# Cross-attention and mixture-of-experts kernel: GpSimd issues only DMAs beside the experts; a new order of the first turn, the router's first step and the late pieces

## The reference

```python
x = x + xattn(layernorm(x), ctx, Wq, Wk, Wv, Wo)
n = layernorm(x)
idx, w = gate(n)                       # top 4 of 32, by groups
x = x + moe(n, idx, w, w1, w2, w3) + (silu(n @ sg) * (n @ su)) @ sd
```

## Time and profile before

| | us |
|---|---|
| median of 3 runs | 1687.53 (1684.35 to 1688.19) |
| profiled execution | 1686.83 |
| its span | 1685.1 |
| PE, DVE, ACT, POOL busy | 1618.0, 1223.4, 787.4, 887.6 |
| TensorE's mean granted clock | 0.991 |

### The profile page before, as it was taken

One profiled execution on the slowest core, in us unless ns is written; L12 is line 12 of the kernel. 1 busy time (PEld: TensorE's weight loads), 2 busy tenths in 40 slices (PEclk: granted clock), 3 DMA queues, 4 the chain that ended last, 5 costly groups with the idle time before them and its releaser, 6 DMA issues. The chain is left out here.

```text
span 1685.1 us, 34839 instructions
## 1 busy us (share of the span) xinstructions
PE 1618.0 (96%) x12194; PEld 1153.3 (68%) x12194; DVE 1223.4 (73%) x3498; ACT 787.4 (47%) x1986; POOL 887.6 (53%) x1188
## 2 busy tenths in 40 slices
PE   6999999999999999999999999999999999999983
PEld 4767677777777777767676767776776766555541
DVE  6887676767676776767676777777777765787872
ACT  5764444435343444444443544445454433565551
POOL 2444544545463636464545463646455356677773
PEclk9999999999999999999999999999999999999997
DMA  7654433344344434343335544445454385799974
GB/s 233 184 143 79 89 80 80 82 76 96 64 96 76 96 61 92 70 102 67 80 74 97 93 95 92 102 95 108 90 112 83 88 319 155 207 281 281 275 194 59
DMA packets 394461, 204.12 MB, mean 121 GB/s; under 512 B 347808, under 2 KB 356000, under 8 KB 394288
## 3 DMA queue, kind: packets, MB, share of 16 engines
q1 hardware_dynamic: 380416, 180.27, 44.4%
q0 software_dynamic: 13312, 20.57, 6.6%
q10 hardware_dynamic: 560, 1.05, 0.2%
HBM read 87.15 MB, written 31.36 MB: 70 GB/s over the span
## 5 line engine op out<-in xcount | busy, mean ns | idle before, releaser
L961 ACT ACTIVATE arena<-arena,neg_max 128x256 f32<-128x256 f32 x512 | 253.7, 496 | 384.7 <-DVE neg_max L1260 331.5
L690 POOL TENSOR_SCALAR arena<-arena,prob_scale 128x256 f16<-128x256 f32 x384 | 184.5, 496 | 461.2 <-DVE prob_scale L1269 447.1
L1260 DVE CUSTOM_DVE_ANT_0 arena<-ps_score,mask_add 128x256 f32<-128x256 f32 x512 | 186.6, 421 | 141.7 <-PE ps_score L1606 141.7
L1604 PE MATMUL ps_query<-xn_both,arena 128*128 128x256 f16 x1024 | 279.2, 273 | 1.6 <-DMA xn_both<-xn_half 1.6
L1606 PE MATMUL ps_query<-xn_both,arena 128*128 128x256 f16 x1024 | 279.1, 273 | 0.0
L1605 PE MATMUL ps_query<-xn_both,arena 128*128 128x256 f16 x1024 | 279.1, 273 | 0.0
L1275 DVE SCALAR_TENSOR_TENSOR arena<-arena,prob_scale 128x256 f16<-128x256 f32 x384 | 233.0, 654 | 8.2 <-POOL arena L690 8.2
L1604 PE MATMUL ps_out<-arena,o_t 128*128 128x512 f16 x512 | 194.1, 379 | 0.7 <-DVE o_t L1280 0.7
L1605 PE MATMUL ps_out<-arena,o_t 128*128 128x512 f16 x512 | 194.0, 379 | 0.0
L1606 PE MATMUL ps_out<-arena,o_t 128*128 128x512 f16 x512 | 194.0, 379 | 0.0
L745 POOL DMA_INDIRECT slot_table<-entry,slot_at x128 | 133.2, 1041 | 48.2 <-issue 33.4
(11 more groups left out here) (319 smaller groups left out, 4110.7 us busy)
## 6 DMA issues: line engine op xcount, KB each, us to landing
arena<-w SPq DMA_DIRECT2D x96, 512.0 KB
x_in<-x SPq DMA_DIRECT2D x16, 512.0 KB, 4.0
xn_rows<-xn_half SPq DMA_DIRECT2D x15, 512.0 KB, 3.1
out_rows_dram<-x SPq DMA_DIRECT2D x30, 256.0 KB
ctx_in<-ctx_t SPq DMA_DIRECT2D x16, 256.0 KB, 3.1
weight_in<-wq SPq DMA_DIRECT2D x8, 512.0 KB, 5.8
weight_in<-wo SPq DMA_DIRECT2D x8, 512.0 KB, 4.6
arena<-arena SPq DMA_TRANSPOSE x256
```

Of the source, the lines that this page charges most:

```text
L690: pool.tensor_scalar(p_rows[:, c, 0, :], probs[:, c, :], prob_scale[:, c:c + 1], 1.0, ALU.mult, ALU.mult).then_inc(norm_hi, 1)
L961: act.activation(probs[:, c, :], probs[:, c, :], ACT.Exp, bias=neg_max[:, c:c + 1], scale=-1.0, accum_out=prob_sum[:, c:c + 1]).then_inc(e ...
L1260: dve.tensor_tensor_reduce(out=probs[:, c, :], in0=ps_score[h][:, t * S:(t + 1) * S], in1=mask_add[b % 2][:, :], scale=-SCORE_SCALE, scala ...
L1604: pe.matmul(dst, a.hi, b.hi, start=start and n == 0, stop=False)
```

## The change

- GpSimd's `expert_high` is gone. ScalarE makes part 2 as well: for experts 0 to 2 among the late pieces, after that as the last thing of turn e for expert e+2, waiting for `pe_ey` (expert_down(e-1)).
- Beside the experts, the hidden tiles of u pieces are split by ScalarE (`piece_high`, after expert_ht_high) and VectorE (`piece_rest`, after expert_ht_low). GpSimd issues only DMAs there.
- `PIECES` has two u pieces in front of each pair of d pieces instead of one. `EARLY` is 24; the 18 others stand in turns 0 to 6, 8 to 14 and 16 to 19, so shared adds 3 and 4 come in turn 8 and 5 and 6 in turn 20 (before: 10 and 26).
- GpSimd's last scatters of batch 14 (`record(z - 1, 1)`) come after its late splits 0 to 5. Piece 23 stands between expert_rows(0) and expert_rows(1).
- Start: x of batch 0 is loaded in two halves with a semaphore each; ctx_low(0) comes after xn_rest; TensorE makes the first value tile before scores(0); VectorE splits value 0 after prob_scales(0), value 1 and context 1 after key_low(1); weight chunks wq 2, wq 3, ... come one place ahead of wo 0, wo 1, ....
- choose_0 and choose_1 of each batch come after key_low(4) instead of around query_low(4).

```diff
@@ PIECES @@
-    PIECES.append(("u", _n, 0))
+    PIECES += [("u", _n, f) for f in range(2)]
     PIECES += [("d", _n - 1, t) for t in range(TB)] if _n else []
-    PIECES += [("u", _n, f) for f in range(1, FSB)]
+    PIECES += [("u", _n, f) for f in range(2, FSB)]
...
-EARLY = 22
+EARLY = 24
-NOT_BY_POOL = (10, 13, 14, 15, 16)
+NOT_BY_POOL = (10, 11, 14, 15, 16)
...
-    if _e % 4 != 3 and EARLY + len(BESIDE) < len(PIECES):
+    if _e % 8 != 7 and EARLY + len(BESIDE) < len(PIECES):
@@ jobs @@
-                by_rows("wo", wo_s, wo, PAIR, D, 0, 0), by_columns("wq", wq_s, wq, KD, 2, 256, 1),
-                by_columns("wv", wv_s, wv, KC, 1, 512, 2), by_rows("wo", wo_s, wo, PAIR, D, 1, 3),
-                by_columns("wq", wq_s, wq, KD, 3, 256, 0), by_columns("wk", wk_s, wk, KC, 1, 512, 1)]
+                by_columns("wq", wq_s, wq, KD, 2, 256, 0), by_rows("wo", wo_s, wo, PAIR, D, 0, 1),
+                by_columns("wv", wv_s, wv, KC, 1, 512, 2), by_columns("wq", wq_s, wq, KD, 3, 256, 3),
+                by_rows("wo", wo_s, wo, PAIR, D, 1, 0), by_columns("wk", wk_s, wk, KC, 1, 512, 1)]
@@ SP @@
+                if b == 0:
+                    for t, sig in ((0, in_first), (1, in_x[0])):
+                        sp.dma_start(x_in[0][:, t, :], x[t * P:(t + 1) * P, :]).then_inc(sig, 16)
+                    return
@@ GpSimd, after the turns @@
-            record(z - 1, 1)
             for k in range(3):
                 late_split(k)
             inv_std(1, z, x1_stats, x1_rstd, x1_normed)
-            for k in (3, 4):
+            for k in (3, 4, 5):
                 late_split(k)
-            for e in range(2):
-                expert_high(e)
-            for k in range(7, 10):
+            record(z - 1, 1)
+            for k in (8, 9):
                 late_split(k)
             add_shared(0)
...
-            expert_high(2)
+            late_split(17)
...
-            for k in range(19, EARLY):
+            for k in (20, 21):
+                late_split(k)
+            for e in range(3, 5):
+                gather(e)
+            for k in (22, 23):
                 late_split(k)
             add_shared(1)
-            for e in range(3, 5):
-                gather(e)
             add_shared(2)
...
             for e in range(E + 2):
-                if e in BESIDE:
-                    late_split(BESIDE[e])
-                if e >= 1 and e - 1 + HELD < E:
-                    expert_high(e - 1 + HELD)
                 if e + 5 < E:
                     gather(e + 5)
@@ ScalarE @@
+            def piece_high(k):
+                kind, n, at = PIECES[k]
+                if kind == "d":
+                    return
+                u, both = ups(n, at), late_h_t[n % 2]
+                act.wait_ge(hid, u + 1)
+                act.wait_ge(glu_lo, u)
+                act.wait_ge(pe_down, downs(n - 1, 0))
+                act.activation(both.hi[:, at, :], late_hidden[at % 2][:, :], ACT.Copy, scale=1.0).then_inc(glu_hi, 1)
...
+                elif part == 2 and e >= HELD:
+                    act.wait_ge(pe_ey, e - HELD + 1)
...
                     expert_ht_high(e)
+                if e in BESIDE:
+                    piece_high(BESIDE[e])
                 if e + HELD < E:
                     expert_high(e + HELD, 1)
                 if e + 2 < E:
                     copy_rows(e + 2)
                 if e >= 2 and e % 2 == 0:
                     scale_y(e - 2)
+                if HELD <= e + 2 < E:
+                    expert_high(e + 2, 2)
@@ VectorE @@
-            ctx_low(0)
             x_norm(0)
             for t in range(TB):
                 xn_rest(0, t)
+            ctx_low(0)
...
                     maxima(i)
-                if i == 0:
-                    value_low(ps_fill[1], 0, 0, 0)
-                    value_low(ps_fill[0], 0, 0, 1)
-                    ctx_low(1)
...
                     piece(1)
+                if i == 0:
+                    value_low(ps_fill[1], 0, 0, 0)
...
-                if j == 3 and routed:
-                    choose_0(z)
                 if i + 1 < TURNS:
                     query_low(i + 1)
-                if j == 3 and routed:
-                    choose_1()
...
                     key_low(i + 1)
+                if i == 0:
+                    value_low(ps_fill[0], 0, 0, 1)
+                    ctx_low(1)
+                if j == 3 and routed:
+                    choose_0(z)
+                    choose_1()
...
                     expert_ht_low(e)
+                if e in BESIDE:
+                    piece_rest(BESIDE[e])
@@ TensorE @@
+                if i == 0:
+                    filler(("value", 0, 0, 0), ps_fill[1])
                 if i < TURNS:
                     scores(i)
                 if i == 0:
-                    filler(("value", 0, 0, 0), ps_fill[1])
                     filler(("value", 0, 0, 1), ps_fill[0])
...
-            for e in range(2):
-                expert_rows(e)
+            expert_rows(0)
+            piece(EARLY - 1)
+            expert_rows(1)
```

More of the change, by code:

```diff
@@ L1486, in dve_program @@
                     find_slots(z)
-                late_head = i < TURNS and first(b, j) is not None and first(b, j)[0] in ("value", "down")
                 if live:
@@ L1492, in dve_program @@
                     piece(1)
+                if i == 0:
+                    value_low(ps_fill[1], 0, 0, 0)
+                late_head = live and first(b, j) is not None and first(b, j)[0] in ("value", "down")
                 if i and not late_head:
@@ L1541, in dve_program @@
             piece(4)
-            for part in (0, 1, 2):
+            piece(5)
+            for part in (0, 1):
                 expert_low(0, part)
@@ L1546, in dve_program @@
             choose_2()
-            piece(7)
             choose_3()
@@ L1580, in dve_program @@
                 table_scaled, 1)
-            piece(21)
+            for k in (21, 22, 23):
+                piece(k)
             for e in range(E + 1):
@@ L1864, in pe_program @@
             rank(ps_fill[1], z)
[L1865 removed]
+            for k in range(11, EARLY - 1):
                 piece(k)
[L1867 to L1868 removed]
+            expert_rows(0)
+            piece(EARLY - 1)
+            expert_rows(1)
             for e in range(E + 1):
```

63 lines of the change are left out of this document (27 added, 36 removed).

## The result

The changed kernel took 1667.7 us (median of 4 runs, 1664.7 to 1669.1) against 1687.2 for the kernel before (1684.4 to 1688.2): ratio 0.9885, 95% interval 0.9866 to 0.9904. Its profiled execution has a span of 1664.9 and a time of 1666.6. Forecast were 1658.3 and 1660.0. Run again beside the experiments it took 1673.0 (6 runs, 1668.8 to 1676.5), ratio 0.9929 (0.9916 to 0.9942), which is 12 us in place of 20: the two intervals don't meet, so the gain is some 0.7% to 1.15%, and no run says more closely which.

What follows compares the result with a forecast made beforehand. TensorE (busy 96%) was taken to bind, GpSimd's chain of adds from turn 20; -3.1 - 6.0 - 0.8 + 6.8 - 23.7 = -26.8 gave time 1660.0, forecast 1661; 50% 1655 to 1668, range 1646 to 1679.

Steps and rivals of the forecast that it cites:

- First turns, -3.1: First batch's opening turns: reordered VectorE splits bring the second scores 3.3 us earlier, the third turn's 3.1; bounds -5.0 to +1.0.
- The part put at nothing, the start: Before the first scores: the earlier first value and x loaded in two halves were each given no gain.
- Router's first step, -6.0: Fourth turns of the last six batches: choose_0 and choose_1 behind the key remove six 1.0 us waits; bounds -6.0 to 0.
- Late pieces, -0.8: Late pieces to first expert: waits and low clock removed, -6.0; two more pieces, +5.2; net -0.8, bounds -3 to +5.
- Turns 0 to 19, +6.8: Expert turns: three more pieces +6.5, a 3.5 us stall gone, new first-turn wait 3.3, ScalarE's order 0.5; bounds 0 to +22.
- Turns 20 to the end, -23.7: Last expert turns, without pieces: 114.3 us becomes 90.5, bound by GpSimd's chain of adds; bounds 80 to 98.
- 9 + 15 + 9.4 + 20.8 + 24.1 + 12.15: Turn 20 to end: gather and even add, shared adds 5 and 6, one, two, three row-add pairs, tail: 90.5 us.
- A: Last expert turns: the adds keep up, TensorE binds to the end, ten us less, 1651; chance 17%.
- B: Expert turns with a piece: ScalarE binds, 0.9 x 18 = 16 us more, 1677; chance 13%.
- C: Experts: DMA engines become the bound, late loads stop ScalarE's tanh, slower at 1694; chance 8%.
- D: Front parts move nothing, as VectorE or transposes' landing replaces each wait: 9 less gained, 1670; chance 8%.
- E: Experts: GpSimd stays as late, held by its DMAs and landings, not the splits: 1676; chance 4%.

Runs made afterwards that it cites:

- e2: Changed kernel with the first turn's value and second-context splits put back ahead of the probability scales: 1674.1 us, ratio 0.9936 to the kernel before.
- e10: Changed kernel with the third part of each expert's weights loading only an eighth of its columns from expert 9 on: 1663.8 us, ratio 0.9879.
- e1: Changed kernel with only the router's first step (choose_0, choose_1) back where it stood: 1676.2 us, ratio 0.9952 to the kernel before.
- e12: e11 with shared add 5 alone in turn 18, add 6 alone in turn 22, and 26 warming matmuls for 18: 1663.3 us, ratio 0.9848.
- e4: Changed kernel with shared adds 1 and 2 ahead of gathers 3, 4 and late splits 22, 23 on GpSimd: 1666.6 us, ratio 0.9886.
- e3: Changed kernel with the third weight part of experts 3 to 31 back on GpSimd: 1674.8 us, ratio 0.9939 to the kernel before.
- e11: Changed kernel with e4's edit and the 18 pieces beside the experts spread, three in four turns, to turn 22: 1659.8 us, ratio 0.9850.
- e9: Changed kernel with VectorE's split of the first context back ahead of the norm of x: 1671.2 us, ratio 0.9923 to the kernel before.

## Why the prediction was right, and where its sizes were off

*What binds* was read rightly, but for the start: the waits named for the other places are those that the profiles show. The second scores' wait is 1.7, the six waits are gone, GpSimd stands 10.2 us behind shared adds 5 and 6, TensorE waits at turn 24, and 11.9 follow the last pair's first add. The sizes were not: the total came near in part because misses cancel. In the first profile turns 0 to 19 cost 5.0 us more than forecast and the end brought 7.3 less, while the start, batches 10 to 15 and the late pieces brought 5.9 more. The first measurement, 1667.7, is at the slow edge of the 1655 to 1668 given one chance in two, the second, 1673.0, is outside it.

*First turns, -3.1*: measured -2.9 to -3.6 for turns 0 and 1, confirmed by e2. The part put at nothing, the start, is not nothing: -1.2 to +2.7, by the context's landing and by a low clock that the trace of before, at 1.00, did not show. Neither was priced; from the key to the first scores it is 6.4 us at full clock (7.6 in e10, with its 2.5 us wait) and 8.1 to 8.9 where the clock fell.

*Router's first step, -6.0*: -7.0, and e1 gives the same 7.0 back: 1.17 a turn, 0.17 more than the wait that the profile showed.

*Late pieces, -0.8*: -2.7 in every profile but e12's (-2.1). Its first term adds up to 3.95 (2.35 + 1.0 + 1.7 - 1.1), not 4.1. The 1.1 us of waits that I left in did not appear, nor did the 0.5 further on.

*Turns 0 to 19, +6.8*: +7.4 to +11.8 with the same code. Three pieces more cost their 6.5 and the stall of turns 14 to 16 is gone, as worked out. The term that was mis-sized is the wait for shared adds 1 and 2: 3.3 expected, 4.9 idle and 3.1 of low clock found (9.5 on ScalarE). I had counted from gather(4); behind it late splits 22 and 23 (1411.68 to 1414.16) stand ahead of the adds, and all four land only 9.2 after they start. And no price was put on the clock that falls behind a wait of 4 us. e4 takes the term away.

*Turns 20 to the end, -23.7*: -9.8 to -16.4. This is the term that failed in size. Against the sum 9 + 15 + 9.4 + 20.8 + 24.1 + 12.15 stand, in the first profile, 13.0 + 15.7 + 9.4 + 23.0 + 24.9 + 11.9 (1567.03, 1580.04, 1595.74, 1605.10, 1628.09, 1652.98, 1664.9). The links without loads and the tail were right within 1 us. The start of shared adds 5 and 6, the sum's first term, was 4 late here, and with the same code it is 12.6 to 20.3 where 9 was forecast: the even add that turn 19 left began 4.9 into turn 20, not 2.4, and the next followed 8.1 behind it, not 6.5. One pair with gathers took 13.2, not 10.4. For both I had taken landings from rows of the end, where the loads had ended. And the gain's cause was put in part in the wrong place: with the casts back on GpSimd e3 still takes 101.9 for this stage where the kernel before takes 114.3, so 12 us of it don't need GpSimd's relief. That they come from where the pieces and shared adds stand is argued, not isolated by a run.

*Rivals.* A did not come: not even without adds 5 and 6. B, ScalarE at its limit, did not either: in turns 3 to 19 TensorE keeps its 7.18 and 8.38, with one wait of 0.8. C's premise is right and its consequence was not: the DMA engines are 0.96 to 1.03 busy from 1490 to 1600 (above), but TensorE never waits for weights there; what they slow is the adds' landing. D is refuted in the first profile by -2.9 in turns 0 and 1 and -7.0 of the router's step. E is right up to turn 20 (e3). On the page "DMA: Bandwidth & Descriptors" of the Trainium skill, section "Anatomy of one DMA", the fit of 2.0 us plus bytes over 436 GB/s gives an estimated 2.6 us for such an add; measured are 3.1 us for the same rows written and 5.1 added, with idle loads, and the sums go by the measured ones.

## What to carry to other kernels

Price a landing by rows of the stage in which it will happen: the same 256 KB add took 5.1 us at the end and 7.9 beside loads, and a chain of 32 is made of these. When an engine is relieved and the chain that it feeds doesn't shorten, the chain was held by what it waits for; spread the filling work over the turns in which the engine that waits for the chain would idle anyway (e11). And take a second profile of the same kernel before an experiment's stage is compared: here one stage varied by 6.6 us with nothing changed. Where a wait on TensorE is forecast, price the slower clock that may follow it too.

## What was not expected of the hardware

- A granted clock of 0.50 in the first queries in most profiles, behind 2.1 to 3.3 us of idle with 5.4 to 6.9 us of warming matmuls before it; behind 0.6 to 1.8 us none, but none either in e10, where 2.5 us of idle came a little later.
- The same load of the context landed at 4.98 to 6.41 us from one execution to the next, and the first key followed 6.3 us behind it each time.
- Adding in place of writing lengthens an indirect DMA of 256 KB by 2.0 us (3.1 to 5.1), and its issue on GpSimd from 0.98 to 1.56 us.
- One program's executions on one chip lie 8 us apart (1668.8 to 1676.5), and by the stage table it is the start, the waits for transposes in batches 10 to 15, and the adds that can make it, each by 4 to 7 us between profiles. The kernel before is not always steadier: beside e9 to e11 its eleven executions lay 9.6 us apart (1680.4 to 1689.9).
